# Decoder layer with linear attention: root of the heads' norm by Newton steps on VectorE, another order from heads to mixing, the product with the norm's weights on GpSimd

## What is computed

```python
w1 = jnp.einsum('bshe,bsed->bshd', Q1, kv1)      # sums over the 16 heads of a token
w2 = jnp.einsum('bshe,bsed->bshd', Q2, kv2)
attn = (1.0 - LAMBDA_INIT) * _rms(w1 - lmb * w2, g2)   # mean square over the 16 of a head
attn = attn.reshape(b, s_len, E)
attn = _rms(attn, g3) + attn                     # mean square over the 256
h = gelu(einsum('bse,fe->bsf', attn, W1))
x = x + einsum('bsf,ef->bse', h, W2) + attn
# _rms(x, g) = x * rsqrt(mean(x * x) + EPS) * g
```

## Time and profile before

| | before |
|---|---|
| median of 3 runs | 704.17 us (703.31 to 706.22) |
| the profiled execution | 704.51 us, span 702.7 us, mean granted clock 0.956 |
| TensorE busy (share) | 634.7 us (90%) |
| VectorE busy | 491.5 us (70%) |
| ScalarE busy | 369.0 us (53%) |
| GpSimd busy | 361.8 us (51%) |

### The profile page before, as it was taken

One profiled execution on the slowest core, in us unless ns is written; L12 is line 12 of the kernel. 1 busy time (PEld: TensorE's weight loads), 2 busy tenths in 40 slices (PEclk: granted clock), 3 DMA queues, 4 the chain that ended last, 5 costly groups with the idle time before them and its releaser, 6 DMA issues.

```text
span 702.7 us, 21603 instructions
## 1 busy us (share of the span) xinstructions
PE 634.7 (90%) x8338; PEld 595.9 (85%) x8338; DVE 491.5 (70%) x1154; ACT 369.0 (53%) x825; POOL 361.8 (51%) x401
## 2 busy tenths in 40 slices
PE   4799798999878957876999999999999999999997
PEld 3677687777677857765999999999999999999997
DVE  5686368586547656856788787788778877886672
ACT  3654366576555735724554455445544554455432
POOL 1212459757847999323356535653565356534322
PEclk9999899799889999997999999999999999999999
DMA  8686655566386646420001101110111011100000
GB/s 268 125 110 95 99 91 114 83 109 105 70 146 194 179 114 170 154 80 26 2 24 39 38 2 39 38 37 0 37 37 37 0 37 37 37 0 16 16 16 31
DMA packets 84140, 50.12 MB, mean 71 GB/s; under 512 B 31321, under 2 KB 83809, under 8 KB 84065
## 3 DMA queue, kind: packets, MB, share of 16 engines
q1 hardware_dynamic: 84064, 49.07, 31.1%
HBM read 23.88 MB, written 12.58 MB: 52 GB/s over the span
## 4 chain that ended last, share of the span: by engine, by line
PE 72%; issue 7%; DVE 7%; POOL 6%; ACT 3%; SPq 2%; DMA 2%; POOLq 0%; DVEq 0%; ACTq 0%
PE banks L694 56%; PE banks L820 4%; PE banks L749 3%; PE banks L838 3%; POOL h_rh L2127 2%; PE banks L979 2%; PE banks L856 2%; POOL m_xa L2057 1%; POOL f_hT_lo L2111 1%; PE banks L763 1%; DMA n_v<-in_L_attn_Wv_dram 1%; DMA m_x<-in_x_dram 1%; SPq L533 1%; ACT h_t L1397 1%; DVE p_st L1554 1%
## 5 line engine op out<-in xcount | busy, mean ns | idle before, releaser
L2111 POOL TENSOR_TENSOR f_hT_lo<-f_hs,f_hT_hi 128x512 fp32r<-128x512 f32 x64 | 87.1, 1362 | 103.5 <-ACT f_hT_hi L1370 99.8
L2127 POOL TENSOR_TENSOR h_rh<-h_ms,mhalf 128x16 f32<-128x16 f32 x32 | 93.9, 2944 | 0.5
L1830 DVE SCALAR_TENSOR_TENSOR f_hs<-banks,nbic,f_h 128x256 f32<-128x256 f32 x128 | 54.6, 479 | 40.6 <-PE banks L694 40.6
L694 PE MATMUL banks<-woT_hi,f_hT_lo 128*128 128x256 f32 x256 | 74.8, 292 | 0.2 <-POOL f_hT_lo L2111 0.2
L694 PE MATMUL banks<-f_adT_hi,lbT_lo 128*128 128x256 f32 x256 | 73.5, 287 | 0.0
L694 PE MATMUL banks<-f_xT_hi,wiT_hi 128*128 128x256 f32 x256 | 73.0, 285 | 0.0
L694 PE MATMUL banks<-f_xT_hi,wiT_lo 128*128 128x256 f32 x256 | 72.8, 284 | 0.0
L694 PE MATMUL banks<-f_xT_lo,wiT_hi 128*128 128x256 f32 x256 | 72.6, 284 | 0.0
L694 PE MATMUL banks<-woT_hi,f_hT_hi 128*128 128x256 f32 x256 | 72.5, 283 | 0.0
L694 PE MATMUL banks<-woT_lo,f_hT_hi 128*128 128x256 f32 x256 | 72.3, 283 | 0.0
L694 PE MATMUL banks<-f_adT_hi,lbT_hi 128*128 128x256 f32 x256 | 72.1, 282 | 0.0
(11 more groups left out here) (262 smaller groups left out, 2029.7 us busy)
## 6 DMA issues: line engine op xcount, KB each, us to landing
h_qk<-p_qk SPq DMA_DIRECT2D x64, 128.0 KB
xin<-in_x_dram SPq DMA_DIRECT2D x16, 256.0 KB, 5.5
h_v<-p_v SPq DMA_DIRECT2D x128, 32.0 KB
attn_scratch<-h_wn SPq DMA_DIRECT2D x16, 256.0 KB, 3.0
m_w<-attn_scratch SPq DMA_DIRECT2D x16, 256.0 KB, 2.8
m_x<-in_x_dram SPq DMA_DIRECT2D x16, 256.0 KB, 3.3
x_scratch<-m_y SPq DMA_DIRECT2D x16, 256.0 KB, 3.2
c_x<-x_scratch SPq DMA_DIRECT2D x16, 256.0 KB, 2.8
```

What stands on the lines that cost most here:

```text
L694: ins = pe.matmul(acc, left(a), right(b), start=first and n == 0, stop=last and n == 2, skip_group_check=skip)
L1830: ins = dve.scalar_tensor_tensor(out=f_hs[:, j % 2, c * T:(c + 1) * T], in0=bank[HB[j]][:, c * T:(c + 1) * T], scalar=nbic[:, f:f + 1], in ...
L2111: pool.tensor_tensor(lo, f_hs[:, j % 2], hi.bitcast(F32), ALU.subtract).then_inc(f_hlo, 1)
L2127: pool.tensor_tensor(h_rh[:, H * i:H * i + H], h_ms[:, H * i:H * i + H], mhalf[:, 0:H], ALU.pow).then_inc(h_rhd, 1)
```

## The change

It has three parts.

1. `head_mean` and `head_rstd` go from GpSimd. `head_newton` on VectorE takes their place: scale and add, a first guess of the root from the bits of the number, and three Newton steps of three instructions. These are eleven instructions on 128 x 64, each of which waits on the semaphore `h_rhd` for the one before.
2. `head_gain` goes from VectorE to GpSimd, unchanged otherwise.
3. The lists of all five engines are written anew. In the loop, `head_newton` (lag 6) stands behind `p_moments` and ahead of `p_elus(3)`, `head_gain` (lag 7) stands on GpSimd behind `p_rstds`, and SyncE stores both halves of w behind `tiles_in(0, 3)` of the next step. Behind the loop many `go` lines change places. `SHARED` is 5 instead of 4.

The diff, cut to its core (a line of "..." stands for what is left out; the ScalarE list has further moves of the same kind):

```diff
+NEWTON = 3
+ROOTS = 2 + 3 * NEWTON
+FIRST_ROOT = float(0x5F3759DF)
...
-        SHARED = 4
+        SHARED = 5
...
@@ SyncE
-            over_all(SU, [(7, store_w(1)), (3, tiles_in(0, 2)), (0, but_first_two(load_x(0))), (3, tiles_in(0, 3)), (3, values_in(0, 0)),
+            over_all(SU, [(3, tiles_in(0, 2)), (0, but_first_two(load_x(0))), (3, tiles_in(0, 3)), (7, store_w(0)),
+                          (7, store_w(1)), (3, values_in(0, 0)), (3, tiles_in(1, 0)), (3, tiles_in(1, 1)),
...
-(6, store_w(0)), (2, tiles_in(0, 1))], 0, WHOLE)
-            go(3, store_w(1))
+                          (2, tiles_in(0, 1))], 0, WHOLE)
...
-            go(7, tiles_in(0, 3), values_in(0, 0), tiles_in(1, 0), tiles_in(1, 1), tiles_in(1, 2), tiles_in(1, 3))
+            go(7, tiles_in(0, 3))
+            go(1, load_mx)
+            go(3, store_w(0), store_w(1))
+            go(7, values_in(0, 0), values_in(0, 1), tiles_in(1, 0), tiles_in(1, 1), tiles_in(1, 2), tiles_in(1, 3))
...
@@ TensorE
+            go(0, turn_attn)
             go(5, head_turn(1), head_turn(2), head_turn(3))
-            go(0, turn_attn)
-            go(6, head_scores(1))
             go(1, turn_attn)
             go(0, hidden)
-            go(7, head_scores(0))
+            go(6, head_scores(1))
             go(2, turn_attn)
             go(1, hidden)
+            go(7, head_scores(0))
...
@@ ScalarE
-            bias_copied()
             go(14, m_gelus)
+            bias_copied()
             go(15, m_gelus)
...
@@ VectorE
             def head_sums(u):
                 dve.wait_ge(h_sqd, nth(u, 1, 1))
                 if u.has(1):
-                    dve.wait_ge(h_msd, nth(u, 1, 0))
+                    dve.wait_ge(h_rhd, nth(u, ROOTS, 0))
...
+            def head_newton(u):
+                def step(ins, k):
+                    ins.then_inc(h_rhd, 1)
+                    dve.wait_ge(h_rhd, nth(u, ROOTS, k))
+                dve.wait_ge(h_ssd, nth(u, 1, 1))
+                if u.has(1):
+                    dve.wait_ge(h_n1d, nth(u, 1, 0))
+                step(dve.tensor_scalar(h_ms[:, :], h_ss[:, :], 1.0 / HD, RMS_EPS, ALU.mult, ALU.add), 1)
+                step(dve.tensor_scalar(h_rh[:, :].bitcast(I32), h_ms[:, :].bitcast(I32), -0.5, FIRST_ROOT, ALU.mult, ALU.add), 2)
+                for n in range(NEWTON):
+                    step(dve.scalar_tensor_tensor(out=h_ss[:, :], in0=h_rh[:, :], scalar=-0.5, in1=h_ms[:, :],
+                                                  op0=ALU.mult, op1=ALU.mult), 3 * n + 3)
+                    step(dve.tensor_tensor(h_ss[:, :], h_ss[:, :], h_rh[:, :], ALU.mult), 3 * n + 4)
+                    step(dve.scalar_tensor_tensor(out=h_rh[:, :], in0=h_ss[:, :], scalar=1.5, in1=h_rh[:, :],
+                                                  op0=ALU.add, op1=ALU.mult), 3 * n + 5)
...
-            over_all(SU, [(4, head_masked(0, 1)), (1, p_moments), (3, p_elus(3)), (2, p_low(0)), (2, p_low(1)),
-(6, head_normal), (6, head_gain), (5, head_sums),
+            over_all(SU, [(4, head_masked(0, 1)), (1, p_moments), (6, head_newton), (3, p_elus(3)), (2, p_low(0)),
+                          (2, p_low(1)), (6, head_normal), (5, head_sums), (2, p_elus(0)),
...
             go(6, head_masked(0, 1))
+            go(4, head_newton)
             go(7, p_elus(3))
-            go(4, head_normal, head_gain)
-            go(5, head_sums)
+            go(4, head_normal)
...
+            go(5, head_sums, head_newton)
...
+            go(0, c_constant)
             go(4, m_residual)
...
             go(7, head_added)
             spread_bias()
...
@@ GpSimd
-            over_all(SU, [(7, head_rstd(2)),(7, head_rstd(3)),(4, p_final(2)),
-                          (4, p_final(3)), (2, p_rstds), (6, head_mean), (6, head_rstd(0)), (3, p_final(0)), (7, head_rthird),
-                          (6, head_rstd(1)), (3, p_final(1)),], FILLED, WHOLE)
-            go(3, head_rstd(2), head_rstd(3))
+            over_all(SU, [(4, p_final(2)), (4, p_final(3)), (2, p_rstds), (7, head_gain), (3, p_final(0)), (7, head_rthird),
+                          (3, p_final(1))], FILLED, WHOLE)
             go(6, p_final(2), p_final(3))
-            go(4, head_mean)
+            go(3, head_gain)
...
-            go(6, head_mean, head_rstd(0), head_rstd(1))
...
-            go(6, head_rstd(2), head_rstd(3), m_with_x)
...
+            go(6, head_gain, m_with_x, head_rthird)
...
-            go(7, head_rstd(0), m_with_x, head_rstd(1), head_rstd(2))
...
+            go(7, head_gain)
             go(9, m_with_x)
+            go(7, head_rthird)
```

More of the change, by code:

```diff
@@ L660, in _ @@
             load_second(6)
+            go(6, store_w(0), store_w(1))
             go(7, store_x1)
-            go(11, load_w)
-            go(6, store_w(0))
-            go(11, load_mx)
-            go(6, store_w(1))
+            go(11, load_w, load_mx)
             go(8, store_x1)
             go(12, load_w, load_mx)
+            go(7, store_w(0), store_w(1))
             go(9, store_x1)
             go(13, load_w, load_mx)
-            go(7, store_w(0), store_w(1))
             go(10, store_x1)
@@ L1927, in _ @@
-            go(0, m_residual)
             go(4, head_added)
             go(1, m_gsplit)
+            go(7, head_masked(0, 0), head_masked(0, 1))
+            clear_gate()
+            go(0, m_residual)
+            go(5, head_sums, head_newton)
             go(3, m_low)
             go(2, m_gsplit)
+            go(5, head_normal)
             go(1, m_residual)
-            go(5, head_normal, head_gain)
+            go(0, c_moments)
             go(4, m_low)
-            go(0, c_moments)
+            go(6, head_sums)
@@ L1936, in _ @@
+            go(7, head_masked(1, 0), head_masked(1, 1))
             go(2, m_residual)
-            go(6, head_sums)
             go(3, m_gsplit)
-            go(7, head_masked(1, 0))
-            go(5, m_low)
-            go(7, head_masked(1, 1))
-            go(5, head_added)
+            go(6, head_newton)
+            go(5, m_low, head_added)
+            go(4, m_gsplit)
             go(3, m_residual)
-            go(4, m_gsplit)
-            go(1, c_moments)
+            go(6, head_normal)
@@ L1946, in _ @@
+            go(0, c_clow)
             go(6, m_low)
+            go(0, c_constant)
             go(4, m_residual)
             go(5, m_gsplit)
+            go(1, c_moments)
+            go(7, m_low)
+            go(0, c_low)
+            go(5, m_residual)
             go(7, head_sums)
-            go(6, head_normal)
-            go(5, m_residual)
-            go(7, m_low)
-            go(6, m_gsplit, head_gain)
+            go(6, m_gsplit)
+            go(7, head_newton)
             go(8, m_low)
-            go(0, c_clow)
@@ L1956, in _ @@
             go(6, m_residual)
             go(7, m_gsplit)
-            go(0, c_constant, c_low)
+            go(6, head_added)
             go(9, m_low)
-            go(7, m_residual)
+            go(7, head_normal, m_residual)
             go(8, m_gsplit)
             go(0, c_usplit)
-            go(6, head_added)
-            go(7, head_normal)
             go(10, m_low)
-            go(7, head_gain)
             go(8, m_residual)
-            go(9, m_gsplit)
             go(0, c_max)
             go(1, c_clow)
-            go(9, m_residual)
+            go(9, m_gsplit)
@@ L1972, in _ @@
             go(11, m_low)
-            go(10, m_gsplit)
             go(7, head_added)
             spread_bias()
+            go(9, m_residual)
+            go(10, m_gsplit)
             go(12, m_low)
+            go(0, c_plow)
+            go(1, c_low)
             go(10, m_residual)
@@ L2112, in remainder, with head_gain @@
                 return emit
-            def head_mean(u):
-                pool.wait_ge(h_ssd, nth(u, 1, 1))
-                if u.has(1):
-                    pool.wait_ge(h_rhd, nth(u, ST, 0))
+            def head_gain(u):
+                if not u.has(1):
+                    pool.wait_ge(s_foldlo, 1)
+                pool.wait_ge(h_n1d, nth(u, 1, 1))
                 apart(pool)
-                pool.tensor_scalar(h_ms[:, :], h_ss[:, :], 1.0 / HD, RMS_EPS, ALU.mult, ALU.add).then_inc(h_msd, 1)
-            def head_rstd(i):
-                def emit(u):
-                    pool.wait_ge(h_msd, nth(u, 1, 1))
-                    if i == 0 and u.has(1):
-                        pool.wait_ge(h_n1d, nth(u, 1, 0))
-                    pool.tensor_tensor(h_rh[:, H * i:H * i + H], h_ms[:, H * i:H * i + H], mhalf[:, 0:H], ALU.pow).then_inc(h_rhd, 1)
-                return emit
+                rows = flat(h_wn[:, u.slot]).rearrange("p (n e) -> p n e", e=HD)
+                pool.tensor_tensor(rows, rows, g2row[:, :].rearrange("p (o e) -> p o e", o=1).broadcast_to([P, ST * H, HD]),
+                                  ALU.mult).then_inc(h_atd, 1)
             def head_rthird(u):
```

179 lines of the change are left out of this document (82 added, 97 removed).

## The result

The changed kernel took **702.64 us** (median of 20 runs, 699.0 to 706.5), the kernel before 705.88 us (20 runs). The ratio is 0.9956, 95% interval 0.9935 to 0.9978: 3.2 us or 0.44% faster, where 13.3 us were forecast. Differences in us are worked out from the ratios, since the kernel before had medians between 704.1 and 707.0 us in the groups of runs.

A forecast was written before the change was run, and what follows sets the result against it. The prediction took GpSimd's in-order queue to bound 242 to about 280 us. Terms -9.8 + 0.5 + 1.0 - 1.5 - 1.0 - 1.0 - 1.5 gave -13.3 us, so 691 us; its own case's range was 686 to 697, overall 683 to 703.

The forecast's parts named there:

- the clock's -1.5: From 242 to 300 us: shorter TensorE waits raise the granted clock from 0.91, -1.5 us (-4 to 0).
- the three orders: Moved list entries: earlier m_aT_lo -1.5 us, bias_copied behind m_gelus(14) -1.0, order from 195 to 242 us -1.0.
- The m_w waits, -9.8: From 242 to 313 us: shorter GpSimd queue cuts TensorE's 12.3 us of m_w waits to 2.5, -9.8 us.
- under 4 was the sign: Sign that the prediction is right: no m_w wait above 2 us and under 4 us in all.
- VectorE in mixing, +1.0 of 0 to 16: From 195 to 300 us: four Newtons less four gains, plus holds by GpSimd, cost +1.0 us (0 to 16).
- The two small terms: Mixing: earlier m_aT_lo -1.5 us (-2.8 to 0); bias_copied moved, so m_g waits less, -1.0 us (-1.1 to 0).
- The term for 195 to 242 us, -1.0 of -3.8 to +3: Last heads beside first mixing: earlier unit 4 pieces against later SyncE loads and head_scores, -1.0 us (-3.8 to +3).
- Newton in the loop, N = 2.75, +0.5: Loop over heads: eleven linked VectorE instructions take 2.75 us a unit, mostly covered, costing +0.5 us (0 to 1.3).
- Rival D: Loop over heads: Newton ahead of p_elus(3) and p_low makes VectorE the bound; slower, 711 us, chance 0.09.
- B: Mixing: c pieces, head_gain and VectorE's longer queue take two thirds of the gain; about -5, 699 us, chance 0.13.
- Rival A: From 242 to 313 us: TensorE's work is the floor, all 19.9 us of idle go, 684 us, chance 0.13.
- Rival C: Mixing: pows only filled time in which sums would wait for m_y or a DMA; 704 us, chance 0.10.

The follow-up runs named there:

- e12: Kernel before with the pows gone, old lists, head_gain still on VectorE, and only Newton's first two instructions on VectorE, no steps: 692.34 us, ratio 0.9823.
- e13: Changed kernel without the nine instructions of the Newton steps, so the root is only a guess: 698.78 us, ratio 0.9897 to the kernel before.
- e2: Kernel before in its old lists, pows replaced by three-step Newton on VectorE, head_gain staying on VectorE: 702.88 us, ratio 0.9956.
- e10: Changed kernel with unit 5's last head_natural earlier on ScalarE, and unit 3's stores and mixing unit 2's load earlier on the DMA queue: 702.87 us, ratio 0.9960.
- e1: Kernel before in its old lists, with three-step Newton on VectorE replacing the pows and head_gain moved to GpSimd: 715.46 us, ratio 1.0153.
- e4: Changed kernel with six Newton steps instead of three: 716.20 us, ratio 1.0158 to the kernel before.
- e17: Kernel before in its old lists, pows replaced by three Newton steps on GpSimd, unit 7's chain behind the sum of mixing unit 7: 694.45 us, ratio 0.9851.

## Why the prediction was wrong

The direction was right, and so was what it said of the pows. The size was four times too large, the time (702.6) lies at the very end of the range, and by the measure set in the prediction this is no change. The forecast of 691 is nearly the time of e12. The runs split the difference in three, each against the run before it:

| step | from, to | ratio | us | forecast |
|---|---|---|---|---|
| root off GpSimd, two instructions on VectorE | before, e12 | 0.9823 | -12.5 | -11.3 |
| `head_gain` to GpSimd and the new lists | e12, e13 | +0.0074 | +5.2 | -3.5 |
| nine Newton instructions a unit | e13, changed | +0.0059 | +4.2 | +1.5 |
| sum | | 0.9956 | -3.1 | -13.3 |

The forecasts are the prediction's terms put to these steps: -9.8 and the clock's -1.5; the three orders; +0.5 and +1.0. The clock and `head_gain`'s 2.5 us inside the -9.8 can't be parted cleanly.

The parts don't simply add. Taken in the other order, by way of e2, the nine instructions cost +9.4 us (e12 to e2), and `head_gain` with the new lists 0.0 (e2 to changed, both 0.9956). In either order two steps of the prediction failed, with 11.4 us between them: the nine instructions (2.7 or 7.9 us more than forecast) and `head_gain` with the lists (8.7 or 3.5 more). They have one thing in common. The prediction looked for what bounds the stretch before, GpSimd's queue, and priced all that takes the pows' place by its length or by idle time in a window; the engines that stand second bound the stretch as soon as GpSimd doesn't.

**The m_w waits, -9.8: right for the pows.** Waits 12.3 to 2.3 us in e12, stretch from unit 0 to 15 shorter by 98.1 - 87.5 = 10.6 us, late sums and GpSimd's queue as read from the earlier trace rows. With -1.5 for the clock (0.91 to 0.97 in e12's window) the two terms of -11.3 answer to e12's -12.5, whose interval reaches 3.4 us to either side. In the changed kernel the waits fell by 6.6 us only, to 5.7 (under 4 was the sign), and most of what is left follows sums that were in time.

**VectorE in mixing, +1.0 of 0 to 16: the first step that failed.** It counted 6 us of work into 37 us of idle time and called it hidden. Idle time in a window is not cover: each Newton instruction stands at the head of VectorE's in-order queue ahead of an m_low that TensorE wants at once. That term measured +4.2 in the new lists and +9.4 in the old ones. The end of 16 covers both; the value was taken from the wrong side. A hold of a Newton step was named too, but by a `head_gain`; the holds that came were by m_xa and the attention pieces beside it, and made unit 6's chain 5.25 us long instead of 2.75. VectorE and GpSimd in the changed kernel:

```profile
236.68 1.28 DVE L1883 TENSOR_SCALAR h_ms<-h_ss 128x64 f32<-128x64 f32 x1
237.99 0.35 DVE L1884 TENSOR_SCALAR h_rh<-h_ms 128x64 int32<-128x64 int32 x1
...
238.63 0.63 DVE L1888 TENSOR_TENSOR h_ss<-h_ss,h_rh 128x64 f32<-128x64 f32 x1
239.30 0.65 DVE L1889 SCALAR_TENSOR_TENSOR h_rh<-h_ss,h_rh 128x64 f32<-128x64 f32 x1
...
241.96 0.69 DVE L1559 TENSOR_TENSOR m_aT_lo<-banks,m_aT_hi 128x512 fp32r<-128x512 f32 x1
```

```profile
236.16 1.74 POOL L2076 TENSOR_TENSOR m_xa<-m_w,m_x 128x512 f32<-128x512 f32 x1
...
239.15 1.40 POOL L2113 TENSOR_TENSOR c_x<-c_x,bvrow 128x256 f32<-128x256 f32 x2
```

Unit 6's Newton takes up VectorE from 236.68 to 241.96, and TensorE waits 3.6 us for the m_aT_lo behind it. Unit 7's, 2.75 us from 257.68, is followed by the other wait, 1.8 us.

**`head_gain` with the lists: the second.** The lists had three terms, -1.5, -1.0 and -1.0, and `head_gain` its length of 2.5 us inside the first term. Together they measured +5.2 without the steps (e12 and e13 ran side by side; their intervals overlap a little, their medians are 6.4 us apart) and 0.0 with them.

- The two small terms took away the waits they named: 2.8 us for the m_aT_lo behind `head_added(7)` and spread_bias, and 1.1 for m_g. Both are gone in the changed kernel; what they saved was not measured apart.
- The term for 195 to 242 us, -1.0 of -3.8 to +3, did not: the stretch from unit 0 to 4 goes from 26.8 (e12) to 29.8 us (e13), and from 4 to 15 nothing changes (60.7 both); the rest lies ahead of m_y of unit 0, where executions scatter. The prediction priced each moved SyncE issue and left out that TensorE's list waits for more than one of them: e10 shows the next wait coming as one goes. Which single piece costs the 2 to 3 us there was not found.
- `head_gain`'s length was right, 2.45 us. Its wait for `head_normal` at the head of GpSimd's queue, with m_xa behind, had no term; e1 prices the move at 14 us in the old lists. How much of the +5.2 is `head_gain` and how much the lists stays open, as no run has one without the other in the new lists.

**Newton in the loop, N = 2.75, +0.5: right in what can be seen.** Unheld links start 0.26 us apart (0.25 forecast), the chain takes 2.73 to 2.91 us in seven of the eight units, and TensorE has no wait for p_xT_lo or p_exp in the loop. Rival D stays out: it needs three more steps (e4) to appear.

Of the rivals, B comes nearest: it named "VectorE's longer queue" and gave 699. It had 0.13. Rival A, 684, was not reached by any run; the best stretch from unit 0 to 15, 86.1 us in e17, is 12.0 us under the kernel before. Rival C is excluded by e12.

## What to carry to other kernels

When a long instruction leaves the engine that bounds a stretch, price what replaces it by its place in the second engine's queue, not by that engine's idle time in a window: here 0.2 to 0.75 of the added length came on the path (4.2, 9.4 and 14 of 18.7 us). Try the replacement on the engine that is being relieved first: a chain of short instructions there (5 to 7 us for 11.8) with one wanted sum put ahead of it gave 10.5 us where moving it away gave 3.1. Try the new place with the old instructions as well, which was not done here. An instruction that waits for another engine, moved to the head of a third queue, delays everything there that has nothing to do with it. And when a change has parts, measure them in both orders: what a part costs here depended on which of the others was already in.
